# Mixture of experts: one sorted list of 71 slots in place of two lists of 39, and expert outputs scattered back to token order

## The reference

```python
x = rmsnorm(src + sa, norm1_w);  flat = x.reshape(S, C)
shared = swiglu(flat @ W_shared_in) @ W_shared_out
# group of 4 experts by argmax of 2 group logits, softmax inside it, top 2 of them
topv, topi = top_k(p_expert, 2);  w = zeros((S, E)).at[arange(S)[:, None], topi].set(topv)
h = swiglu(flat @ W1_shared)                  # (S, 512), one hidden row for a token
for e in range(8):
    routed = routed + h @ W2_experts[e] * w[:, e:e + 1]
return src + rmsnorm(x + shared + routed, norm2_w)    # the outer residual is x5
```

## Time and profile before

| | us |
|---|---|
| median of 3 runs | 5847.61 |
| lowest and highest | 5835.81, 5856.86 |
| the profiled execution's own time | 5839.69 |
| its span in the trace | 5837.6 |
| first DMA of stage_moe | 5174.95 |
| first transpose of the slot loop | 5574.66 |
| last result copied from PSUM | 5773.15 |
| last VectorE operation | 5831.34 |

### The profile page before, as it was taken

How to read it: one execution, slowest core, us unless ns; L and a number is a source line. 1 busy time by engine, 2 the same in 40 slices (tenths; PEclk the granted TensorE clock), 3 DMA queues, 4 the chain that set the end, 5 groups by cost and what they waited for, 6 DMA issues and landing times. The chain is left out here.

```text
span 5837.6 us, 139849 instructions
## 1 busy us (share of the span) xinstructions
PE 5046.7 (86%) x53868; PEld 3302.1 (57%) x53868; DVE 3899.9 (67%) x6903; ACT 3133.8 (54%) x4732; POOL 2458.5 (42%) x2096
## 2 busy tenths in 40 slices
PE   7688888888798889788889989997889999989994
PEld 3455555555487544377778778885532333346674
DVE  5899999999796955544444434444689888844424
ACT  5899999999654845422222223333445666642221
POOL 1778787788565623343444432112530000001114
PEclk9899999999999999889999989998798999999997
DMA  5202020020111133422323321112652222232256
GB/s 169 50 17 53 14 49 21 26 36 13 39 45 51 54 132 154 163 95 99 105 101 107 107 96 63 46 51 54 164 147 43 45 46 46 44 97 68 77 161 188
DMA packets 441106, 457.16 MB, mean 78 GB/s; under 512 B 227874, under 2 KB 376728, under 8 KB 432272
## 3 DMA queue, kind: packets, MB, share of 16 engines
q1 hardware_dynamic: 418704, 397.99, 24.1%
q0 software_dynamic: 8192, 25.17, 1.3%
q10 hardware_dynamic: 13568, 25.17, 1.2%
HBM read 276.38 MB, written 171.82 MB: 77 GB/s over the span
## 5 line engine op out<-in xcount | busy, mean ns | idle before, releaser
L538 POOL TENSOR_SCALAR attn_u<-attn_rel,attn_aux 128x1024 f32<-128x1024 f32 x512 | 1088.5, 2126 | 267.6 <-DVE attn_nm L565 267.5
L689 PE MATMUL attn_tp<-attn_ident,attn_pr 128*128 128x128 f32 x4096 | 571.0, 283 | 242.8 <-ACT attn_pt L628 240.8
L3366 DVE TENSOR_REDUCE attn_mx<-attn_mp 128x1 f32<-128x512 f32 x1024 | 652.6, 685 | 91.7 <-PE attn_mp L3445 90.7
L689 PEld LDWEIGHTS attn_tp<-attn_ident,attn_pr 128*128 128x128 f32 x4096 | 446.7, 143 | 463.2 <-ACT attn_pt L628 325.7
L557 DVE SCALAR_TENSOR_TENSOR attn_u<-attn_rel,attn_aux,attn_u 128x1024 f32<-128x1024 f32 x512 | 681.6, 1331 | 26.6 <-POOL attn_u L538 18.0
L3430 ACT ACTIVATE attn_pt<-attn_st 128x1024 f32<-128x1024 f32 x512 | 506.5, 1022 | 283.3 <-PE attn_st L3456 282.7
L649 ACT ACTIVATE attn_pr<-attn_pr,attn_nm 128x1024 f32<-128x1024 f32 x512 | 603.6, 1179 | 85.4 <-DVE attn_nm L565 85.3
L565 DVE CUSTOM_DVE_ANT_0 attn_pr<-attn_u,attn_s 128x1024 f32<-128x1024 f32 x512 | 619.5, 1210 | 42.0 <-PE attn_s L680 30.5
L628 ACT ACTIVATE attn_pt<-attn_tp 128x512 f32<-128x512 f32 x1024 | 566.6, 623 | 8.1 <-issue 5.2
L3445 PE MATMUL attn_mp<-attn_kt,attn_qt 96*128 96x512 bf16 x1024 | 371.9, 394 | 17.6 <-DMA attn_qt<-s_q 16.6
L680 PE MATMUL attn_s<-attn_kt,attn_qt 96*128 96x512 bf16 x1024 | 315.5, 391 | 50.6 <-DMA attn_kt<-s_k 23.8
(11 more groups left out here) (549 smaller groups left out, 10720.0 us busy)
## 6 DMA issues: line engine op xcount, KB each, us to landing
s_qkv<-gin_qkv SPq DMA_DIRECT2D x32, 1536.0 KB, 5.0
core_qk<-s_qkv SPq DMA_DIRECT2D x32, 1024.0 KB, 5.0
attn_qt<-s_q SPq DMA_DIRECT2D x384, 64.0 KB, 3.0
attn_kt<-s_k SPq DMA_DIRECT2D x192, 128.0 KB, 4.2
moe_rows<-s_hid_s SPq DMA_DIRECT2D x78, 256.0 KB, 2.8
core_arow<-s_alr SPq DMA_DIRECT2D x32, 512.0 KB
core_grow<-s_gar SPq DMA_DIRECT2D x32, 512.0 KB, 3.6
core_vv<-s_qkv SPq DMA_DIRECT2D x32, 512.0 KB, 3.5
```

What stands on the lines that cost most here:

```text
L538: pool.tensor_scalar(u[:, x % 4], rel[:, z % 2, 1], aux[:, s, 4 + NH + h:5 + NH + h], aux[:, s, 4 + 2 * NH + h:5 + 2 * NH + h], ALU.mult, ...
L689: ins = pe.transpose(tp[k][:, n], pr[:, x % BUF, (4 * k + n) * P:(4 * k + n + 1) * P], ident[:])
L3366: dve.reduce_max(mx[w % 2][:].rearrange("p h t a -> p (h t a)")[:, j:j + 1], bank(("row", number))[:], AX.X).then_inc(m["max_done"], 1)
```

## The change

One sorted list replaces the two: `HALF` becomes all 16 pairs, the list has 71 slots, and `tables` and `pad` run once, after the last pair. Padding is shared between SP (experts 0 to 3) and ScalarE (experts 4 to 7). A second, narrow list `tag_s` with two numbers in a row (8 bytes) is sorted along with `hid_s`: the place of the result in token order (`token + 4096 k`), and the token's weight. GpSimd scatters it by an indirect DMA beside each scatter of hidden rows. In the slot loop SP loads the 128 tags of a slot beside its rows, VectorE turns the first number into an index (`home`) and multiplies the result by the second while it copies it out, and GpSimd scatters the 128 result rows to `y_t`, in token order. The closing work of all 16 pairs follows the last slot: SP loads `y_t` by plain DMAs of 256 rows (two a pair), and VectorE adds them without weights, 512 elements wide. The index computation for the gathers (`gidx`) goes. At the start SP waits for two small constants, then writes 7 x 128 zero rows and as many tags.

```diff
-    HALF = PAIRS // 2
-    HT = TILES // 2
+    HALF = PAIRS
+    HT = TILES
-        LAST = 2 * SL
+        LAST = SL
-            def pad(h):
+            def pad(h, experts):
                 sp.wait_ge(m["table_done"], h + 1)
-                for n in range(NE):
+                for n in experts:
...
+                    sp.dma_start(d["tag_s"][bass.ds(row, P), :], spare[:, h, n]).then_inc(m["pad_out"], 16)
             def load_rows(s):
...
                 need(sp, "tb_mm", s - 3)
...
                 sp.dma_start(rows[:, s % 4], d["hid_s"][bass.ds(row, P), :]).then_inc(e["row_in"][s % 4], 16)
-            def store_rows(s):
...
-                sp.wait_ge(m["y_copy"], s + 1)
-                sp.dma_start(d[f"y_s{h}"][at_:at_ + P, :], yb[:, s % 3]).then_inc(e["y_out"][s % 3], 16)
+                need(sp, "y_copy", s - 3)
+                sp.dma_start(tags[:, s % 4], d["tag_s"][bass.ds(row, P), :]).then_inc(e["row_in"][s % 4], 16)
+            def load_results(c):
...
+                        sp.wait_ge(e["y_out"][n], 16 * ((LAST - n + 2) // 3))
+                need(sp, "acc2", c - 3)
+                for k in range(TOPK):
+                    at_ = k * T + c * 2 * P
+                    sp.dma_start(g[:, c % 4, k], d["y_t"][at_:at_ + 2 * P, :].rearrange("(z p) c -> p z c", p=P)).then_inc(e["g_in"][c % 4], 16)
             def load_x5(c):
                 need(sp, "out_done", c - 1)
...
+            sp.wait_ge(m["tag_in"], 32)
...
+                sp.dma_start(d["hid_s"][at_:at_ + 7 * P, :].rearrange("(n p) c -> p n c", p=P),
+                             zero[:].rearrange("p (o c) -> p o c", o=1).to_broadcast([P, 7, HID])).then_inc(m["zero_out"], 16)
+                sp.dma_start(d["tag_s"][at_:at_ + 7 * P, :].rearrange("(n p) c -> p n c", p=P), spare[:, h, NE:]).then_inc(m["zero_out"], 16)
-                if s >= 1:
-                    store_rows(s - 1)
-                if tail(s) and tail(s)[1] == 0:
-                    load_x5(tail(s)[0])
+            for c in range(PAIRS):
+                load_results(c)
+                if c >= 2:
+                    load_x5(c)
+                        pool.indirect_dma_start(d["tag_s"], bass.IndirectOffsetOnAxis(idx[:, t, k:k + 1], 0), tag[:, t, k], None
+                                                ).then_inc(e["tag_out"][t % 2], 16)
+            def results(s):
+                pool.wait_ge(m["home_done"], s + 1)
+                pool.wait_ge(m["y_copy"], s + 1)
+                pool.indirect_dma_start(d["y_t"], bass.IndirectOffsetOnAxis(home[:, s % 3], 0), yb[:, s % 3], None).then_inc(e["y_out"][s % 3], 16)
             def copy_out(s):
-                dve.wait_ge(m["ob_mm"], s + 1)
+                dve.wait_ge(e["row_in"][s % 4], 32 * (s // 4) + 32)
...
+                dve.tensor_copy(home[:, s % 3], tags[:, s % 4, 0:1]).then_inc(m["home_done"], 1)
+                dve.wait_ge(m["ob_mm"], s + 1)
+                dve.tensor_scalar(yb[:, s % 3], ub[s % 2][:, 0:D], tags[:, s % 4, 1:2], None, ALU.mult).then_inc(m["y_copy"], 1)
             def gathered(c):
...
+                dve.tensor_tensor(both, both, g[:, c % 4, 0], ALU.add).then_inc(m["acc1"], 1)
+                dve.wait_ge(m["acc1"], c + 1)
+                dve.tensor_tensor(both, both, g[:, c % 4, 1], ALU.add).then_inc(m["acc2"], 1)
             def turn_rows(s):
-                pe.wait_ge(e["row_in"][s % 4], 16 * (s // 4) + 16)
+                pe.wait_ge(e["row_in"][s % 4], 32 * (s // 4) + 32)
-SLOTS = T // 128 + 7
-REGION = T // 2 + P
+SLOTS = 2 * T // 128 + 7
+REGION = T + P
```

More of the change, by code:

```diff
@@ L3587, in steps @@
                 yield i, i + 1 if i + 1 < PAIRS else None
-        def tail(s):
-            n = s - SL - 4
-            c, k = n // 4, n % 4
-            return (c, k) if 0 <= c < HALF else None
         @block.sync
@@ L3618, in load_rows @@
                         sp.wait_ge(e["sc_out"][n], 32 * HT * (h + 1) // 4)
-                    sp.wait_ge(m["pad_out"], 16 * NE * (h + 1))
+                    for n in range(2):
+                        sp.wait_ge(e["tag_out"][n], 32 * HT * (h + 1) // 2)
+                    sp.wait_ge(m["pad_out"], 32 * NE * (h + 1))
                     if h == 0:
@@ L3661, in _ @@
                     load_pair(nxt + 1)
-                if i == HALF + 1:
-                    pad(0)
+            pad(0, range(NE // 2))
             for s in range(3):
@@ L3719, in _ @@
                     scatter(i)
-            for h in range(2):
-                for n in range(3):
-                    pool.wait_ge(e["y_out"][n], 16 * (h + 1) * SL // 3)
-                pool.wait_ge(m["gidx_done"], h + 1)
-                for c in range(h * HALF, h * HALF + HALF):
-                    gather(c)
-                    if c > h * HALF:
-                        last_root(c - 1)
-                last_root(h * HALF + HALF - 1)
+            for s in range(LAST):
+                results(s)
+            for c in range(PAIRS):
+                last_root(c)
         @block.vector
@@ L3878, in gathered @@
                     dve.wait_ge(m["acc0"], PAIRS)
-                for k, name in enumerate(("acc1", "acc2")):
-                    for z in range(2):
-                        t = 2 * c + z
-                        if k == 0:
-                            dve.wait_ge(e["g_in"][t % 4], 32 * (t // 4) + 32)
-                        else:
-                            dve.wait_ge(m["acc1"], t + 1)
-                        dve.scalar_tensor_tensor(acc[:, t], g[:, t % 4, k], wsel[:, t, k:k + 1], acc[:, t], ALU.mult, ALU.add).then_inc(m[name], 1)
+                dve.wait_ge(e["g_in"][c % 4], 32 * (c // 4) + 32)
+                both = acc[:, 2 * c:2 * c + 2]
+                dve.tensor_tensor(both, both, g[:, c % 4, 0], ALU.add).then_inc(m["acc1"], 1)
+                dve.wait_ge(m["acc1"], c + 1)
+                dve.tensor_tensor(both, both, g[:, c % 4, 1], ALU.add).then_inc(m["acc2"], 1)
             def last_variance(c):
@@ L3928, in _ @@
                 copy_out(s)
-                if tail(s):
-                    c, k = tail(s)
-                    if k == 1:
-                        gathered(c)
-                    if k == 2:
-                        last_variance(c)
-                    if k == 3:
-                        last_norm(c)
-            for c in range(HALF, PAIRS):
+            for c in range(PAIRS):
                 gathered(c)
-                if c > HALF:
+                if c > 0:
                     last_norm(c - 1)
@@ L3975, in copy_rows, with pad @@
                 act.activation(rt[:, s % 2].rearrange("p k n -> p (k n)"), ua[s % 2][:], ACT.Copy).then_inc(m["rt_c"], 1)
+            def pad(h, experts):
+                act.wait_ge(m["table_done"], h + 1)
+                for n in experts:
+                    row = act.value_load(pads[0:1, h, n:n + 1], min_val=0, max_val=SORTED - P)
+                    act.dma_start(d["hid_s"][bass.ds(row, P), :], zero[:]).then_inc(m["pad_out"], 16)
+                    act.dma_start(d["tag_s"][bass.ds(row, P), :], spare[:, h, n]).then_inc(m["pad_out"], 16)
             def last_squares(c):
@@ L4000, in _ @@
                     copy_x(nxt)
+            pad(0, range(NE // 2, NE))
             for s in range(LAST):
                 copy_rows(s)
-                if tail(s):
-                    c, k = tail(s)
-                    if k == 2:
-                        last_squares(c)
-                    if k == 0 and c:
-                        store(c - 1)
-            store(HALF - 1)
-            for c in range(HALF, PAIRS):
+            for c in range(PAIRS):
                 last_squares(c)
-                if c > HALF:
+                if c > 0:
                     store(c - 1)
@@ L4182, in layout @@
     out["moe_off"] = np.repeat(region[:, None], 2, axis=1).astype(np.float32)
+    tag = np.zeros((P, TILES, 2, 2), np.float32)
+    tag[..., 0] = np.arange(P)[:, None, None] + P * np.arange(TILES)[None, :, None] + T * np.arange(2)[None, None, :]
+    out["moe_tag"] = tag
+    spare = np.zeros((P, 2, 15, 2), np.float32)
+    spare[..., 0] = 2 * T + np.arange(P)[:, None, None] + P * np.arange(30).reshape(1, 2, 15)
+    out["moe_spare"] = spare
     out["moe_slot"] = np.arange(SLOTS, dtype=np.float32)
```

64 lines of the change are left out of this document (23 added, 41 removed).

## The result

| | before | after |
|---|---|---|
| median, us (20 runs each) | 5835.8 | 5855.35 |
| lowest and highest | 5824.68, 5856.86 | 5837.4, 5871.34 |
| ratio, 95% interval | | 1.0033 [1.0023, 1.0043] |
| profiled execution's own time | 5839.69 | 5867.73 |
| its span | 5837.6 | 5865.9 |

The change is slower, by 0.33%, some 19.5 us, with the interval wholly on that side of no change. The forecast was a gain of 3.8 us, that is no difference; the time lies inside the range. The profiled execution after lies 12.4 above its median, that before 3.9, and 15.4 of the 28 us between the two spans lie ahead of the stage, where the two programs are the same. Over all profiles taken of the two kernels the stage begins between 5173.3 and 5183.3 before and between 5176.0 and 5190.4 after; those two ranges overlap, and nothing ahead of the stage differs.

What follows compares the result with a forecast made beforehand. The last stage's end was taken as the sum of pair loop, seams, slots and closing work. 2 - 0.8 + 0 - 21 + 16 = -3.8 us gave 5835.9 profiled, 5844 us on the median's scale; range 5826 to 5869.

Steps and rivals of the forecast that it cites:

- What bounds the kernel: Last stage: its end is set by pair loop, first seam, slots, last seam and closing work, all altered by the change.
- Start, +2 (0 to +4.5): Start of the stage: constants, zero blocks and tag rows delay pair 2's inputs by 7.0 to 12.4 us, less 8 slack.
- Border, -0.8: Border of the halves: TensorE's wait for the counts of half 0 goes, saving 0.8 us.
- Tag scatters, 0: Pair loop: four more indirect DMAs a pair on GpSimd, 5 us in a pair of 24, cost nothing.
- First seam, 0: Padding behind the pair loop: the first multiply still starts at about 5596.1, with three slots fewer left; 0 us.
- Slot loop, -21: Slot loop: without closing work between slots the pitch is 2.165 us and the last multiply ends at 5752; 21 us saved.
- The rival of the late tags: Slot loop: tags land after their 3.47 us lead and slow it; a 4.5 us landing adds 24 us, 5868; chance 0.2.
- Closing work, +16: Behind the last slot: load bursts hold VectorE to 4.25 us a pair; 74.6 us behind the last copy, 58.9 before.
- The rival of an even pace at 3.25: Closing work: loads land in 3.4 us or less and VectorE sets 3.25 us a pair; 5832 us; chance 0.15.
- The end: From VectorE's last operation to the end of the span: forecast 0 change.
- "Nothing else moves": Rival: low clock after the seam lasts longer, or burst loads take 7 us, or both; 5855 to 5860; chance 0.1.

Runs made afterwards that it cites:

- r7: The changed kernel with SP's wait for constants, the zero blocks and their tags moved behind the inputs of pairs 2 and 3; 1.0014 to before.
- r2: The changed kernel with the tag list filled once, early, from a constant in long rows, so padding writes no tags; 1.0009 to before.
- r14: The same kernel as r2 in one more execution; seam 21.0 us, stage 666.0 us.
- r9: r2 with the 64 indirect DMAs that scatter tags also left out; 0.9997 to before.
- r1: The changed kernel run again, unchanged; median 5875.05 us, pair loop 369.0 us, stage 692.5 us.
- r8: The changed kernel with the edits of r2, r5, r6 and r7 together; 5826.79 us, 0.9965 to before.
- r5: The changed kernel with eight tag buffers in place of four; 1.0019 to before.
- r6: The changed kernel with SP loading the results three pairs ahead, in front of x5; 1.0012 to before.
- r3: The changed kernel with each padding block of tags written a second time, to a list nobody reads; 1.0061 to before.
- r4: The changed kernel with SP issuing the padding of all eight experts and ScalarE none; 1.0036 to before.

## Why the prediction was wrong, point by point

- **What bounds the kernel** held: the end was set by the sum of pair loop, seam, slots, seam and closing work, and every piece could be read by itself.
- **Start, +2 (0 to +4.5):** +3.2 in the mean, in range. The place was the one named: r7 moves wait, zeros and tags away, and pair 2 no longer waits. But the parts were not weighed right. The 896 small rows were put "at nothing up to 2.8 us", and they are 2.3 of the 3.2 (r2, r14 and r9, which keep the wait and the zeros, stand at 44.2 in the mean). The rate of 310 GB/s for a full share wasn't a ceiling either: r2's seam moved 381 GB/s at 1.01 (5596 to 5598).
- **Border, -0.8:** -1.3 in the first profile, +0.8 in the mean of those without r1. Too small to be told.
- **Tag scatters, 0:** held within some 3.5 us (r9).
- **First seam, 0: this step failed.** The table (6.2 for 6.3) and the way from landing to multiply (6.5) were right. Two terms were not. A second DMA an expert made the pitch 2.2 where "some 1.5" was put, 2 us; and "2.6 until all has landed" was 10.44, 8 us. The error has a form: the landing was taken from rows of transfers that had no short rows beside them, and the 1024 rows of 8 bytes were given no time, though the same text gave the 896 at the start an upper bound. With even that bound, 50 ns a row, the seam would have had +3 in it. And 3.4 of the 8 us are a wait with no transfer under way, for which the sum had no term at all. Where the 8-byte rows are gone (r2, r14, r8), the seam is 20.9 to 21.0, within 0.7 of the forecast's 21.6.
- **Slot loop, -21:** the loop took 161.0 to 164.7 for 155.9. The rival of the late tags was there in kind: lead 3.26 for 3.47, and r5 removes it all. Its size was between the two cases. The forecast asked for the median landing (2.4, under the lead), the rival for one of 4.5 in every slot; in truth single landings, up to 4.3, stall single slots. A lead 1 us above the median is no cover for the slow ones, and such stalls are not made up.
- **Closing work, +16:** +14.6 in the mean. The burst of loads and the cycle over two pairs are as read: 3.28 and 4.87, 8.15 for two where 8.5 was forecast, and r6 takes it away. The rival of an even pace at 3.25 fell. VectorE's own pace was put at 3.25 and is 2.98 (r6), but it didn't bind here. The Trainium skill ("DMA: Bandwidth & Descriptors", section "Anatomy of one DMA — SWDGE (gpsimd) path"), by whose fit the prediction estimated 4.4 us for 1 MB, would have given 3.75 a pair; the measured pitch, 4.08, lies between that and the 4.25 of the sum.
- **The end:** no term; 2.1 us.
- **"Nothing else moves":** the low clock behind the longer seam didn't last longer. The first multiply took 3.77, the next is back at the pitch of 2.17.

In the mean of four profiles each the forecast's -3.8 became +19.3 by 16.7 of seam and slot part together, 1.2 at the start, 2.1 at the end and 4.6 in the pair loop (3 of them r1's), less 1.4 in the closing work. The two largest, seam and slot loop, both come with the side list of short rows: once by its writes, once by loads with a lead too short. The forecast gave a slowdown of over 0.3% a chance of 0.21. That the total still fell inside the stated range was luck in part: the range was wide for late tags at 4.5 us in every slot, and the seam, which made the larger share, had 2 us each way.

## What to carry to other kernels

When a narrow side list is padded at a seam, count its rows by number, not by bytes: here a block of 128 rows of 8 bytes lengthened the seam by 0.6 to 1.5 us (eight rows an engine at 0.08 to 0.18), as much as a block of 128 rows of 2 KB takes or twice that. Where it can be filled early in long rows, its padding costs nothing at the seam. And for a load with a tight lead compare the lead with the slowest landings, not with the median: a few bytes more of buffer bought 5 to 9 us here. Two lists with a seam between were a cover for each other's serial part; merging them saved slots and cost that cover, and of the kernels tried only the one with all four repairs gained on the kernel before.

## What the runs showed of the hardware that was not expected

- Blocks of 128 rows of 8 bytes written between blocks of zeros lengthened the seam by 0.08 to 0.18 us for each row an engine had. The short rows took 9 ns (median) in the transfer records; the 2 KB rows beside them rose from 86 to 180 ns.
- Behind such writes the last landing came 3.1 to 4.3 us after the last transfer had ended, with a DMA share of 0.00 (after, r3, r4); without them 0.3 us (r2).
- At 5603 to 5607 a DMA share of 1.38 moved 112 GB/s; in r2's seam a share of 1.01 moved 381.
- Loading 1 KB in 128 rows of 8 bytes, one block at a time beside full rows, landed in 2.4 us (median), no later than the rows; but up to 4.3.
- Two DMAs and a register load on one queue had a pitch of 2.2 us, with two queues at it; on SP alone it was 1.87 (5606.71 to 5608.58), and the register load's part of it fell from 0.90 to 0.54.
- The end of the program, behind the last operation of an engine, grew from 5.6 to 7.7 us along with GpSimd's indirect DMAs, from 128 to 199.
